# Histogram tiles of the edge ranking: 5 of every 16 written by ScalarE

## The reference

```
xn = _layernorm(x, axis=-1)
x = x + _L0_gnn_ref(xn, edge_index, ...) + _L0_mix_ref(xn[None], ...)[0]
x = x + _L0_ffn_ref(_layernorm(x, axis=-1)[None], ...)[0]
...
```

## Time and profile before

| | |
|---|---|
| median of three runs | 7658.55 us |
| the profiled execution | 7664.92 us |
| its span, first to last instruction | 7662.9 us |
| busy in the span | PE 5795.8 us (76%), DVE 4051.7 (53%), POOL 3059.9 (40%), ACT 2728.5 (36%) |
| mean granted TensorE clock | 0.819 |
| `rank_edges` | from the start to about 723 us |
| histogram, order 0 | 19.70 to 134.73 us |
| histogram, order 1 | 360.70 to 475.73 us |

### The profile page before, as it was taken

How to read it: one execution, slowest core, us unless ns; L and a number is a source line. 1 busy time by engine, 2 the same in 40 slices (tenths; PEclk the granted TensorE clock), 3 DMA queues, 4 the chain that set the end, 5 groups by cost and what they waited for, 6 DMA issues and landing times. The chain is left out here.

```text
span 7662.9 us, 89136 instructions
## 1 busy us (share of the span) xinstructions
PE 5795.8 (76%) x21954; PEld 3657.7 (48%) x21954; DVE 4051.7 (53%) x9873; ACT 2728.5 (36%) x7590; POOL 3059.9 (40%) x3137
## 2 busy tenths in 40 slices
PE   5564677777995788876976788996888848997486
PEld 3332454443552566542545553553655525564243
DVE  7876456663112899965245334215566675556401
ACT  2534366661220344410114432111555515554010
POOL 1775444533772665610007750000455505553101
PEclk9999777677997877878988888897776666987597
DMA  2534211110001555510013330001333314333122
GB/s 89 159 91 146 53 31 37 37 24 27 2 2 42 167 160 159 159 35 13 0 57 106 105 71 23 0 0 42 85 87 93 93 41 112 98 98 80 56 101 73
DMA packets 268797, 547.49 MB, mean 71 GB/s; under 512 B 86992, under 2 KB 136588, under 8 KB 263948
## 3 DMA queue, kind: packets, MB, share of 16 engines
q0 software_dynamic: 134496, 314.63, 16.4%
q1 hardware_dynamic: 133932, 228.62, 9.5%
HBM read 493.99 MB, written 49.00 MB: 71 GB/s over the span
## 5 line engine op out<-in xcount | busy, mean ns | idle before, releaser
L1463 POOL DMA_INDIRECT L3a_edges_rows<-scratch_L3a,L3a_edges_index x416 | 404.4, 972 | 905.3 <-DMA L3a_edges_last<-order_dst_last 525.7
L1463 POOL DMA_INDIRECT L_edges_rows<-scratch_L_kv,L_edges_index x416 | 506.8, 1218 | 430.7 <-PE L_edges_ps_sum L1708 197.1
L632 POOL DMA_INDIRECT L_edges_rows<-scratch_L,L_edges_index x416 | 393.3, 945 | 572.7 <-SPq L616 446.3
L1463 POOL DMA_INDIRECT L_edges_rows<-scratch_L,L_edges_index x416 | 407.9, 981 | 530.4 <-DVE L_edges_msg L1510 293.6
L1463 POOL DMA_INDIRECT L3b_edges_rows<-scratch_L3b,L3b_edges_index x416 | 399.5, 960 | 393.2 <-PE L3b_edges_ps_sum L1708 225.4
L482 POOL DMA_INDIRECT scratch_by_dst<-dst_record,dst_dest x400 | 439.6, 1099 | 271.5 <-DVE dst_dest L334 150.1
L2505 DVE TENSOR_TENSOR L_experts_gated_h<-L_experts_hidden,L_experts_ps_g 128x800 f32<-128x800 f32 x112 | 110.6, 988 | 665.7 <-PE L_experts_ps_g L2458 665.7
L1584 DVE TENSOR_TENSOR L_acc<-L_edges_ps_sum,L_acc 128x264 f32 (+1 forms) x832 | 357.0, 429 | 156.9 <-PE L_edges_ps_sum L1708 91.9
L482 POOL DMA_INDIRECT scratch_by_src<-src_record,src_dest x400 | 383.1, 958 | 124.0 <-issue 121.7
L2496 ACT ACTIVATE L_experts_hidden<-L_experts_ps_h,L_eb_sb 128x400 f32<-128x400 f32 x320 | 190.2, 594 | 647.7 <-PE L_experts_ps_h L2451 647.7
L1708 PE MATMUL L3a_edges_ps_sum<-L3a_edges_rows,L3a_edges_hot 128*128 128x264 f32 x832 | 375.8, 613 | 2.1 <-DVE L_acc L1584 2.1
(11 more groups left out here) (771 smaller groups left out, 13174.8 us busy)
## 6 DMA issues: line engine op xcount, KB each, us to landing
x<-scratch_dst_key_rows SPq DMA_DIRECT2D x50, 512.0 KB, 4.6
x<-scratch_src_key_rows SPq DMA_DIRECT2D x50, 512.0 KB, 5.0
L_experts_w<-in_L_w SPq DMA_DIRECT2D x16, 1024.0 KB
L_edges_rows<-scratch_L,L_edges_index POOLq DMA_INDIRECT x832
L_edges_lo_rows<-order_src_lo_rows SPq DMA_DIRECT2D x52, 256.0 KB
L3a_edges_lo_rows<-order_dst_lo_rows SPq DMA_DIRECT2D x52, 256.0 KB
L3b_edges_lo_rows<-order_dst_lo_rows SPq DMA_DIRECT2D x52, 256.0 KB
x<-scratch_dst_lo_rows SPq DMA_DIRECT2D x50, 256.0 KB, 3.6
```

The lines of the kernel that those rows point to most:

```text
L632: pool.indirect_dma_start(rows[:, n % RING, k, :], None, row_table, bass.IndirectOffsetOnAxis(index[:, t:t + 1].bitcast(U32), 0)).then_inc ...
L1463: pool.indirect_dma_start(rows[:, n % RING, k, 0:RW], None, row_table, bass.IndirectOffsetOnAxis(index[:, t:t + 1].bitcast(U32), 0)).then_ ...
```

## The change

Of every group of 16 tiles `hot_lo`, VectorE writes the first 11 and ScalarE the last 5 (ACT_TILES). ScalarE computes a tile in two steps: the absolute value of `lo - iota` for each of five tiles (input in f32, output in bf16), and then one Relu of 1 less that over all five at once, in place, 640 columns. A semaphore `hot_apart` stands between the two, and `hot_act` tells of the finished five. This code isn't a loop on the engine: it is written out, 25 groups of 6 instructions for each order. On TensorE the last five matmuls of a group have a second wait, for `hot_act`. ScalarE's tiles come after the copies of the key rows and ahead of the first distance.

```
+ACT_TILES = 5
...
                     with dve.Fori(0, ET // SU) as i:
                         v.tensor_tensor(hot_hi[:, ds(i * SU, SU), :], bcast(hi_f[:, ds(i * SU, SU)], NT, 2),
                                         bcast(kit.iota[:, 0:NT], SU, 1), ALU.is_equal).then_inc(hot[o], 1)
-                        for u in range(SU):
+                        for u in range(SU - ACT_TILES):
                             ins = v.tensor_scalar(hot_lo[:, ds(i * SU + u, 1), :].squeeze(1), iota_b[:],
                                                   lo_f[:, ds(i * SU + u, 1)], None, ALU.is_equal)
                         ins.then_inc(hot[o], 1)
...
                     with pe.Fori(0, ET // SU) as i:
                         for u in range(SU):
                             pe.wait_ge(hot[o], i * 2 + 2)
+                            if u >= SU - ACT_TILES:
+                                pe.wait_ge(hot_act[o], i + 1)
                             nc.tensor.matmul(ps_run[:, 0:NT], hot_lo[:, ds(i * SU + u, 1), :].squeeze(1),
                                              hot_hi[:, ds(i * SU + u, 1), :].squeeze(1), start=False, stop=True,
                                              skip_group_check=True)
...
+                    act.wait_ge(cast[o], 1)
+                    if o:
+                        act.wait_ge(counted[0], BATCHES)
+                    for i in range(ET // SU):
+                        for u in range(SU - ACT_TILES, SU):
+                            ins = nc.scalar.activation(hot_lo[:, ds(i * SU + u, 1), :].squeeze(1), kit.iota[:], ACT.Abs,
+                                                       scale=-1.0, bias=lo_f[:, ds(i * SU + u, 1)])
+                        ins.then_inc(hot_apart[o], 1)
+                        act.wait_ge(hot_apart[o], i + 1)
+                        here = hot_lo[:, ds(i * SU + SU - ACT_TILES, ACT_TILES), :]
+                        nc.scalar.activation(here, here, ACT.Relu, scale=-1.0, bias=kit.ones[:, 0:1]).then_inc(hot_act[o], 1)
```

More of the change, by code:

```diff
@@ L181, in rank_edges @@
         counted, high, split, chosen, selected, placed, recorded = ({} for _ in range(7))
+        hot_apart, hot_act = {}, {}
         for o in range(2):
-            for at_, what in ((cast, "cast"), (hot, "hot"), (histogram, "histogram"), (totals, "totals"),
+            for at_, what in ((cast, "cast"), (hot, "hot"), (hot_apart, "hot_apart"), (hot_act, "hot_act"), (histogram, "histogram"), (totals, "totals"),
                               (prefix, "prefix"), (based, "based"), (begins, "begins"), (rowed, "rowed"),
```

## The result

The changed kernel is slower: 7687.69 us, median of six runs (7681.36 to 7701.74), against 7660.84 us for the kernel before (six runs, 7658.23 to 7669.0). The ratio is 1.0037, with a 95% interval of 1.0024 to 1.0049. The forecast was 7670.0 and the range ended at 7677.0, so the sign was right and the loss more than twice too small. The profiled execution took 7681.36 us (span 7679.3, 16.4 us more than that of before), less than the medians are apart (26.9). It is the fastest of the six, so its trace holds 16.4 us of a loss that the median puts at 26.9; that gap is the real question of this study.

The account below looks back on a forecast made before the run. TensorE's instruction stream was taken to bound the histogram; five added instructions a group cost 13.7 us less 0.5, 13.2 per order, +11.4 on the stage, making 7670.0 us from 7658.55. Range 7662 to 7677.

Parts of the forecast that it names:

- What bounds the histogram: Histogram: TensorE's register instructions hold it at 4.48 us a group, while VectorE needs 3.36 and already waits for it.
- TensorE's second wait: Last five matmuls of a histogram group: five added instructions of 0.11 us each, 13.2 us net per order.
- From the order to the stage: Ranking stage: GpSimd starts 13.2 us later, scatters faster beside an idle VectorE, so the stage ends 11.4 us later.
- Beyond the barrier everything is shifted as it stands: All stages after the ranking: they only start later, so the sum stays +11.4 us.
- third rival: Histogram: VectorE is the bound after all, so the stage ends up to 21 us earlier, 7637.5; chance 0.02.

Follow-up runs that it names:

- pe_written_out: Kernel before with TensorE's histogram loop written out and one wait a group instead of sixteen, VectorE writing all 16 tiles: 7649.93 us against 7666.47, ratio 0.9978.
- both_written_out: Changed kernel with TensorE's histogram written out, one wait a group for each of VectorE and ScalarE: 7622.05 us against 7666.47 for the kernel before.
- waits_only: Changed kernel with VectorE writing all 16 tiles, ScalarE none, the five second waits kept but always satisfied: 7681.51 us, ratio 1.0024 to the kernel before.
- act_only: Changed kernel with VectorE writing all 16 tiles, no second wait, ScalarE's tiles into an unread buffer: 7665.1 us against 7665.49 for the kernel before.
- no_relief: Changed kernel plus five unread VectorE comparisons a group: ratios 1.0033 and 1.0058 to the kernel before, in two sessions with slow transfers.
- The three repeats: Changed kernel, unedited, in three further sessions: 7708.46, 7699.39 and 7695.33 us against 7665.49, 7666.47 and 7663.5 for the kernel before.
- repeat_2: Changed kernel, unedited, measured a third time: 7699.39 us against 7666.47 for the kernel before, ratio 1.0038.
- one_wait: Changed kernel with the second wait ahead of the twelfth matmul of a group alone: 7672.06 us, ratio 1.0009 to the kernel before.
- waits and work together: Changed kernel with VectorE writing all 16 tiles, ScalarE's tiles going unread, TensorE's five waits kept: 7684.91 us against 7663.5 for the kernel before.
- the delay made otherwise: Changed kernel with one second wait a group, plus 18 loop turns of zero matmuls on TensorE after each histogram: 7686.32 us, ratio 1.0026 to the kernel before.

## Why the prediction was wrong

*What bounds the histogram* was right: groups of 5.0 us forecast and 5.02 measured, the copy near 147.9 and at 146.96, ScalarE's 2.4 us a group and 2.33, its Relu 0.82 us and 0.827. Experiments pe_written_out and both_written_out bear out the cause that it named, TensorE's register instructions and not the array, by taking them away (with the waits on one value, as said there). VectorE's wait was 61.26 us where 57 were forecast, since its group shrank by 1.04 us (3.36 to 2.32) and not by 0.84: the 0.17 us in which it stood idle before each wide comparison are gone too. That reaches no one on the path.

*TensorE's second wait* was right in its shape, four EVENT_SEMAPHOREs and one ALU_OP that carries the first wait, and nearly in its price, 0.104 us for the 0.11 taken; an order lost 12.6 and 13.3 us for 13.2 forecast. waits_only against act_only shows that the whole stage's loss is this term.

*From the order to the stage* was too small by 2.4 us: 11.4 forecast, 13.8 measured. GpSimd started 12.2 us late instead of 13.2 and was to win 1.8 us back. It won nothing: 150.31 to 711.60 us before and 162.53 to 723.80 after are both 561.3 us. In the other traces at the usual speed of transfers the 400 scatters took up to 565.5, with VectorE relieved or not, so 1.8 us is less than they vary by. The last scatter thus ended 12.2 us later, 0.8 more than the sum has.
```profile
L199 DVEq COMPARE_BRANCH  x1: 47/47/47, 700.6 to 700.6; - x1
...
L199 POOLq COMPARE_BRANCH  x1: 38/38/38, 712.8 to 712.8; - x1
```

```profile
L203 POOLq COMPARE_BRANCH  x1: 38/38/38, 726.5 to 726.5; - x1
L203 DVEq COMPARE_BRANCH  x1: 47/47/47, 726.7 to 726.7; - x1
L203 POOLq DRAIN  x1: 9202/9202/9202, 726.7 to 726.7; - x1
```

The first is the end of the stage before, the second the end after, where VectorE's branch and the drain come at the same time. That is chance: the drain doesn't wait for VectorE. In no_relief, where VectorE needed until 1129.8 us, it began right behind GpSimd's branch all the same:

```profile
L204 POOLq COMPARE_BRANCH  x1: 38/38/38, 783.9 to 783.9; - x1
L204 POOLq DRAIN  x1: 9202/9202/9202, 784.1 to 784.1; - x1
...
L204 DVEq COMPARE_BRANCH  x1: 47/47/47, 1129.8 to 1129.8; - x1
```

VectorE is thus to be measured against the end of the drain, as the prediction did when it gave order 1 some 21.8 us to spare, and in the changed kernel it has some 9 us left (726.7 to 735.9).

*The step that failed* is "Beyond the barrier everything is shifted as it stands". It put the rest of the program, 90% of the span, at nothing: the sum has no term for it, and the range 2.7 us (7674.3 to 7677). The runs showed 13 us there, the 26.9 between the medians less the 13.8 of the stage, more than the whole loss forecast. The three repeats showed 16 to 28 by the same reckoning. The profile had a warning: a mean clock of 0.819 beside a clock of 1.00 in the ranking itself, so that later stages live on a clock that isn't granted in full.

What stands in the step's place is known in part. Executions with a low mean clock took 22 us more, and the traces of repeat_2 and one_wait show a stretch of layer 3 that takes 12 to 14 us longer at a lower clock. In the three repeats 10 of 18 executions were of that kind. In the six runs of the forecast's own comparison, only one was (7701.74 at 0.815); the other five took 7687.1 us on the mean, 25 us above the mean of the kernel before, 7661.8. So the low clock explains little of the 26.9, and some 11 us of it have no cause that a run shows. Over all 24 executions, those with the usual clock lost 19 to 20 us for a stage of 14 to 16, some 5 us beyond it.

Nor was it shown what makes the whole change draw the low clock more often than its waits alone. Of the 36 executions of the waits alone, of waits and work together and of the delay made otherwise, 3 were at 0.815 or lower; of those of act_only 2 of 11, of one_wait 3 of 12, of pe_written_out 3 of 8, of both_written_out 2 of 5. The numbers are too small to rank them.

## What to carry to other kernels

Before an engine is relieved, look at who waits for whom at the end of the stage: here the relieved engine already stood idle for 23 us. A second wait in a loop on an engine whose sequencer is full cost an instruction, 0.104 us here, even when it was satisfied each time, so a wait for the same value belongs ahead of the first use alone: with that edit the kernel was 6.6 us above before (one_wait), against 43.0 for the whole change in the same session. With one such wait a group the same split of the tiles lost 6.6 us beside a TensorE that computed its operand addresses in a loop, and won 28 beside one whose histogram was written out.

## What was not expected of the hardware

- Sixteen pairs of weight load and matmul at 25 columns took 0.61 us with fixed addresses (0.029 us apart) and 3.90 us with computed ones (0.248 apart), at the same clock of 1.00; the first had one wait and the second sixteen. The prediction's third rival reckoned with 1.3 us for them.
- The time of a program of which the first tenth was changed varied by up to 40 us from one execution to the next (7672.8 to 7712.4 among 24). The eleven with a mean granted clock of 0.812 to 0.815 took 22 us more than the others on the mean. One profiled execution is then no measure of the change: the three first traces said +16.4, +7.9 and +40.6 us.
- GpSimd's drain behind its 400 scatters took 9.2 us in every trace and began 0.1 to 0.2 us after GpSimd's own last branch, whether VectorE was done or not. Where the stage ended with GpSimd, the next one waited for it.
